# Router logits in a decoder layer: the tokens as the stationary operand, the eight router columns as the moving one

## The chip, the cores and the metric

The kernel runs on one core of one Trainium2 chip. The metric is the device time of one execution in microseconds (us). The core has a matrix engine (TensorE, PE in the rows; its weight loads are listed apart as PEld), a vector engine (VectorE, DVE), a scalar engine (ScalarE, ACT), GpSimd (POOL) and a sync engine (SyncE, SP) whose queue issues the transfers here. TensorE's array runs at one of two clocks, 1.2 or 2.4 GHz; the profile gives the granted clock as a share of full speed, 0.5 or 1.0.

A matmul on TensorE has a stationary operand, which a weight load (LDWEIGHTS) puts into the array, and a moving operand, whose columns stream through it.

## The reference

The reference is one decoder layer over 64 sequences of 128 tokens, 256 wide: self-attention and a norm, cross-attention and a norm, then a mixture of eight experts and a norm. The change lies in the first step of the mixture, the router's logits. There are 8192 tokens, and every token gets eight logits:

```python
N = B * T
x = x_btd.reshape(N, Dm)
cap = int(math.ceil(CF * N / E))
probs = jax.nn.softmax(x @ Wr + br, axis=-1)
gates, ids = jax.lax.top_k(probs, K)
```

`Wr` is 256x8 and `br` has 8 elements, all in float32. The two largest probabilities of a token pick its experts; each expert takes at most `cap` tokens, those with the largest gates.

## The kernel before

The program is a row of blocks, each with a program of its own for every engine and a common end: the attention layers (`attention_layers`), the logits (`logits_block`), the routing (`route_block`), the experts (`experts_block`) and the last norm (`norm_block`). A block starts when the one before it has ended on all engines, so what one block gains or loses in time is passed on to the end of the program unless a later one waits for something else.

`logits_block` takes the 8192 rows in 16 groups of 512 tokens (`G`), four tiles of 128 (`NB`). SyncE loads a group as a tile `x2` of 128 x 4 x 256 floats (512 KB); `LOADS` is the number of buffers, and load g waits until TensorE has transposed group g - LOADS (`t_full`). For each group g TensorE does three things:

- eight transposes (L845, `lg_T<-lg_ident,lg_x`), so that the features of a token lie across partitions. ScalarE and VectorE copy the two halves out of PSUM into `xT` (L866 and L885, 512 columns each);
- the logits, turned round (L825, `lg_L<-lg_xT,lg_wr`): the router's weight half `wr[:, t, :]`, eight columns, is stationary, and the 512 transposed tokens move; the two halves accumulate in `lb`, 8 partitions x 512. VectorE adds the bias, one number for each partition, and writes `lT` (L878);
- the way back (L834, `lg_B<-lg_ident,lg_lT`): four transposes of 8 x 128 that bring `lT` to 128 tokens x 8 logits in `bb`. ScalarE copies these 128x32 into `logits` (L861).

The order on TensorE is written out by hand as a pipeline: the transposes of group g, the logits of group g - 1 (`logits_of`), the way back of group g - 2 (`back`). TensorE works through its instructions in this order, and begins only when the two constants, `ident` and `wr`, and the bias are in (`const_in`). A matmul in float32 leaves two records in the trace, each with its own weight load, so a logits step of two matmuls has four; a transpose leaves one.

Of the kernel before, what the change touches and what calls it, by code (L numbers as in the profile page):

```python
# [4 lines left out]
FP32 = mybir.dt.float32  # L5
BF16 = mybir.dt.bfloat16
FP32R = mybir.dt.float32r
ALU = mybir.AluOpType
# [3 lines left out]
P = 128  # L12
# [3 lines left out]
NB = 4  # L16
G = NB * P
HALVES = D // P
# [745 lines left out]
E = 8  # L764
# [6 lines left out]
def logits_block(nc, tiles, rows_dram, sum_dram, wr_dram, br_dram, ident_dram, logits):  # L771


    groups = tiles // NB
    LOADS = 4
    with ExitStack() as c:
        ident = c.enter_context(nc.sbuf_tensor("lg_ident", [P, P], FP32))
        wr = c.enter_context(nc.sbuf_tensor("lg_wr", [P, HALVES, E], FP32))
        br = c.enter_context(nc.sbuf_tensor("lg_br", [E, 1], FP32))
        zero = c.enter_context(nc.sbuf_tensor("lg_zero", [P, D + E], FP32))  # L780
        x2 = c.enter_context(nc.sbuf_tensor("lg_x2", [P, LOADS, NB, D], FP32))
        xT = c.enter_context(nc.sbuf_tensor("lg_xT", [P, 2, HALVES, G], FP32))
        lT = c.enter_context(nc.sbuf_tensor("lg_lT", [E, 2, G], FP32))
        tb = [c.enter_context(nc.psum_tensor(f"lg_T{i}", [P, G], FP32)) for i in range(4)]
        lb = [c.enter_context(nc.psum_tensor(f"lg_L{i}", [E, G], FP32)) for i in range(2)]
        bb = [c.enter_context(nc.psum_tensor(f"lg_B{i}", [P, NB, E], FP32)) for i in range(2)]
        const_in = c.enter_context(nc.semaphore("lg_const_in"))
        x_loaded = [c.enter_context(nc.semaphore(f"lg_x_loaded{i}")) for i in range(LOADS)]
        zero_made = c.enter_context(nc.semaphore("lg_zero_made"))
        zeroed = c.enter_context(nc.semaphore("lg_zeroed"))  # L790
        t_full = c.enter_context(nc.semaphore("lg_t_full"))
        a_copied = c.enter_context(nc.semaphore("lg_a_copied"))
        d_copied = c.enter_context(nc.semaphore("lg_d_copied"))
        l_full = c.enter_context(nc.semaphore("lg_l_full"))
        l_done = c.enter_context(nc.semaphore("lg_l_done"))
        b_full = c.enter_context(nc.semaphore("lg_b_full"))
        b_done = c.enter_context(nc.semaphore("lg_b_done"))
        block = c.enter_context(nc.Block())

        @block.sync  # L800
        def _(sp):
            sp.dma_start(ident[:], ident_dram).then_inc(const_in, 16)
            sp.dma_start(wr[:], wr_dram.rearrange("(t p) n -> p t n", p=P)).then_inc(const_in, 16)
            sp.dma_start(br[:], br_dram.rearrange("(p a) -> p a", a=1)).then_inc(const_in, 16)
            for g in range(groups):
                if g >= LOADS:
                    sp.wait_ge(t_full, g - LOADS + 1)
                sp.dma_start(x2[:, g % LOADS], rows_dram[g * G:(g + 1) * G, 0:D]
                             .rearrange("(b p) n -> p b n", p=P)).then_inc(x_loaded[g % LOADS], 16)
            sp.wait_ge(zero_made, 1)  # L810
            sp.dma_start(rows_dram[groups * G:groups * G + P, :], zero[:]).then_inc(zeroed, 16)
            sp.dma_start(sum_dram[groups * G:groups * G + P, :], zero[:, 0:D]).then_inc(zeroed, 16)
            sp.wait_ge(zeroed, 32)

        @block.tensor
        def _(pe):
            pe.wait_ge(const_in, 48)

            def logits_of(g):
                pe.wait_ge(a_copied, g + 1)  # L820
                pe.wait_ge(d_copied, g + 1)
                if g >= 2:
                    pe.wait_ge(l_done, g - 1)
                for t in range(HALVES):
                    last = nc.tensor.matmul(lb[g % 2][:, :], wr[:, t, :], xT[:, g % 2, t, :],  # L825
                                            start=(t == 0), stop=(t == HALVES - 1))
                last.then_inc(l_full, 1)

            def back(g):
                pe.wait_ge(l_done, g + 1)  # L830
                if g >= 2:
                    pe.wait_ge(b_done, g - 1)
                for n in range(NB):
                    last = nc.tensor.matmul(bb[g % 2][:, n, :], lT[:, g % 2, n * P:(n + 1) * P], ident[0:E, 0:E],  # L834
                                            start=True, stop=True, is_transpose=True)
                last.then_inc(b_full, 1)

            for g in range(groups):
                pe.wait_ge(x_loaded[g % LOADS], 16 * (g // LOADS + 1))
                if g >= 2:  # L840
                    pe.wait_ge(a_copied, g - 1)
                    pe.wait_ge(d_copied, g - 1)
                for half in range(HALVES):
                    for n in range(NB):
                        last = nc.tensor.matmul(tb[2 * (g % 2) + half][:, n * P:(n + 1) * P],  # L845
                                                x2[:, g % LOADS, n, half * P:(half + 1) * P], ident[:],
                                                start=True, stop=True, is_transpose=True)
                last.then_inc(t_full, 1)
                if g >= 1:
                    logits_of(g - 1)  # L850
                if g >= 2:
                    back(g - 2)
            logits_of(groups - 1)
            back(groups - 2)
            back(groups - 1)

        @block.scalar
        def _(act):
            def take(g):
                act.wait_ge(b_full, g + 1)  # L860
                nc.scalar.copy(logits[:, g * NB:(g + 1) * NB, :], bb[g % 2][:, :, :]).then_inc(b_done, 1)  # L861
            for g in range(groups):
                act.wait_ge(t_full, g + 1)
                if g >= 2:
                    act.wait_ge(l_full, g - 1)
                nc.scalar.copy(xT[:, g % 2, 0, :], tb[2 * (g % 2)][:, :]).then_inc(a_copied, 1)  # L866
                if g >= 2:
                    take(g - 2)
            take(groups - 2)
            take(groups - 1)  # L870

        @block.vector
        def _(dve):
            def add_bias(g):
                dve.wait_ge(l_full, g + 1)
                if g >= 2:
                    dve.wait_ge(b_full, g - 1)
                nc.vector.tensor_scalar(lT[:, g % 2, :], lb[g % 2][:, :], br[:, 0:1], None, ALU.add).then_inc(l_done, 1)  # L878
            nc.vector.memset(zero[:], 0.0).then_inc(zero_made, 1)
            dve.wait_ge(const_in, 48)  # L880
            for g in range(groups):
                dve.wait_ge(t_full, g + 1)
                if g >= 2:
                    dve.wait_ge(l_full, g - 1)
                nc.vector.tensor_copy(xT[:, g % 2, 1, :], tb[2 * (g % 2) + 1][:, :]).then_inc(d_copied, 1)  # L885
                if g >= 1:
                    add_bias(g - 1)
            add_bias(groups - 1)
# [693 lines left out]
def moe(nc, tokens, cap, ins, rows, total, lists, out):  # L1582
    tiles = tokens // P
    with ExitStack() as c:
        logits = c.enter_context(nc.sbuf_tensor("logits", [P, tiles, E], FP32))
        logits_block(nc, tiles, rows, total, ins["wr"], ins["br"], ins["ident"], logits)
        route_block(nc, tiles, cap, logits, rows, lists, ins)
    experts_block(nc, cap, rows, lists, total, {k: ins[k] for k in ("w1", "w2", "b1", "b2")}, ins)
    norm_block(nc, tiles, total, out)
# [92 lines left out]
```

## Time and profile before

| | us |
|---|---|
| median of three runs | 1737.83 (1737.78 to 1737.97) |
| the profiled execution | 1737.31 |
| its span in the trace | 1735.6 |
| first load of x in the logits block issued | 983.28 |
| first transpose of the block | 987.07 |
| last write of logits begins | 1041.00 |
| first work of the routing block on VectorE | 1041.63 |

The page of the profile gives the whole span: TensorE is busy for 84% of it, VectorE for 61%, ScalarE for 56%. These shares mix stages with different limits. The logits block is about 3% of the span, and only its own stretch, from 982 to 1042 us, is read in what follows. Views used: the page; the timeline, which merges instructions of one kind in a row (start, duration of the merged piece, engine, line, operation, tile written <- tiles read, count, and in brackets the idle time before it and what ended it); the view of one tile's instructions; and the busy time of every engine by stretch with the granted clock. The durations of matmul records are modelled and contain the way through the array, so the spacing of their starts tells the rate, not their duration.

### The profile page before, as it was taken

Reading aid. Unit: us, or ns where it says so; the run is one execution under the profiler, and the core shown is the slowest. Engines: PE = TensorE matmul, PEld = TensorE weight load, DVE = VectorE, ACT = ScalarE, POOL = GpSimd, SP = SyncE. Lnnn points to the kernel's source line nnn. Section 1 sums busy time; section 2 is a strip of 40 time slices with the busy share of each in tenths; the row PEclk is TensorE's granted clock in tenths of the full one; section 3 lists DMA queues with packets and bytes.
Section 4 is the critical chain, followed back from the end, with each engine's and each line's share of the span. In section 5 each row is a group of like instructions: output and inputs, shape, how many; then the busy total and the mean of one; then the engine's idle time right before and its main releaser. Section 6 shows DMA issues by size and latency. Waiting matters only on the chain. (4 is left out here: it accounts for less than half of the span.)

```text
span 1735.6 us, 43611 instructions
## 1 busy us (share of the span) xinstructions
PE 1463.6 (84%) x17896; PEld 1214.8 (70%) x17896; DVE 1054.5 (61%) x2277; ACT 970.5 (56%) x1419; POOL 632.2 (36%) x615
## 2 busy tenths in 40 slices
PE   5999999999999999999998591223999999999950
PEld 4777777777777777777776341223999999999950
DVE  3666666666667677767766347794544454455425
ACT  3677767777766666676765220012655555555507
POOL 1544444444432222322230000055254455454326
PEclk9999999999999999999999795555999999999985
DMA  5011112112112222222111341004334433442229
GB/s 178 20 57 57 57 57 63 58 56 68 45 52 67 75 75 75 74 74 75 63 60 38 126 116 12 0 0 134 83 58 96 97 81 61 96 98 45 28 53 357
DMA packets 129795, 129.54 MB, mean 75 GB/s; under 512 B 28288, under 2 KB 116464, under 8 KB 129600
## 3 DMA queue, kind: packets, MB, share of 16 engines
q1 hardware_dynamic: 114496, 106.29, 19.6%
q0 software_dynamic: 15104, 20.48, 7.1%
q8 instruction: 143, 2.34, 0.5%
q14 instruction: 52, 0.43, 0.1%
HBM read 82.54 MB, written 44.20 MB: 73 GB/s over the span
## 5 line engine op out<-in xcount | busy, mean ns | idle before, releaser
L495 ACT ACTIVATE at_pr<-at_A 128x2048 f32<-128x2048 f32 x128 | 240.7, 1880 | 196.4 <-PE at_A L325 196.4
L587 DVE TENSOR_REDUCE at_mx<-at_A 128x12 f32<-128x1536 f32 x128 | 224.6, 1755 | 32.7 <-PE at_A L292 27.1
L34 PE MATMUL ex_D<-ex_w,ex_hT 128*128 128x256 f32 (+1 forms) x1920 | 233.8, 281 | 0.4
L34 PEld LDWEIGHTS ex_D<-ex_w,ex_hT 128*128 128x128 f32 (+1 forms) x1920 | 230.5, 184 | 3.1 <-DVE ex_raw L1426 1.9
L34 PE MATMUL ex_U<-ex_xT,ex_w 128*128 128x384 f32 (+1 forms) x1152 | 222.1, 352 | 0.0
L1482 POOL DMA_INDIRECT total<-ex_o,ex_ids x80 | 131.6, 1645 | 228.0 <-DVE ex_o L1431 196.3
L34 PEld LDWEIGHTS ex_U<-ex_xT,ex_w 128*128 128x128 f32 x1152 | 207.2, 189 | 7.4
L716 POOL TENSOR_SCALAR_AFFINE_SELECT at_pr<-at_pr 128x2048 f32<-128x2048 f32 x64 | 128.5, 2008 | 225.2 <-ACT at_pr L495 225.2
L1416 DVE TENSOR_TENSOR ex_hT<-ex_h,ex_hT 128x384 fp32r<-128x384 f32 (+1 forms) x192 | 112.6, 587 | 97.0 <-ACT ex_hT L1376 97.0
L623 DVE TENSOR_TENSOR at_oT<-at_C,at_oT 128x512 fp32r<-128x512 f32 x64 | 44.3, 692 | 178.0 <-ACT at_oT L508 178.0
L325 PE MATMUL at_A<-at_qp,at_kt 32*128 32x256 f32 x2048 | 142.5, 392 | 0.0
L341 PE MATMUL at_C<-at_pr,at_v 128*32 128x128 f32 x4096 | 139.2, 277 | 1.0 <-ACT at_oq L502 1.0
L341 PEld LDWEIGHTS at_C<-at_pr,at_v 128*32 128x32 f32 x4096 | 104.6, 110 | 43.7 <-issue 42.4
L1375 ACT ACTIVATE ex_h<-ex_U,ex_b 128x384 f32<-128x384 f32 (+1 forms) x192 | 116.7, 608 | 25.5 <-PE ex_U L34 21.4
L707 POOL TENSOR_TENSOR at_sT<-at_turned,at_sT 128x1024 fp32r<-128x1024 f32 x32 | 75.8, 2369 | 126.7 <-ACT at_sT L451 126.7
L1376 ACT ACTIVATE ex_hT<-ex_U,ex_b 128x384 fp32r<-128x384 f32 (+1 forms) x192 | 115.2, 600 | 0.0
L1466 POOL DMA_INDIRECT ex_xg<-rows,ex_ids x80 | 102.1, 1276 | 35.2 <-issue 22.6
L1348 ACT CAST ex_xT<-ex_T 128x384 fp32r<-128x384 f32 (+1 forms) x48 | 21.9, 510 | 165.4 <-PE ex_T L1299 165.4
L723 POOL TENSOR_SCALAR at_shift<-at_mv 128x2 f32<-128x2 f32 x64 | 14.8, 231 | 269.5 <-DVE at_mv L649 266.9
L34 PE MATMUL at_B<-at_wo,at_oT 128*128 128x256 f32 x768 | 108.1, 290 | 1.9 <-DVE at_oT L623 1.4
L34 PE MATMUL at_B<-at_sT,at_wk 128*128 128x512 f32 x384 | 105.8, 411 | 1.4 <-ACT at_qp L464 1.4
L34 PE MATMUL at_B<-at_wv,at_sT 128*128 128x256 f32 x768 | 106.7, 288 | 0.0
(189 smaller groups left out, 2703.3 us busy)
## 6 DMA issues: line engine op xcount, KB each, us to landing
ex_w_in<-in_w SPq DMA_DIRECT2D x16, 1024.0 KB, 6.8
at_turned<-in_x_turned SPq DMA_DIRECT2D x16, 512.0 KB, 4.0
at_x<-in_x SPq DMA_DIRECT2D x16, 512.0 KB, 3.7
x<-at_y SPq DMA_DIRECT2D x32, 256.0 KB, 2.2
at_x<-x SPq DMA_DIRECT2D x16, 512.0 KB, 3.7
at_turned<-in_ctx_turned SPq DMA_DIRECT2D x16, 512.0 KB, 4.1
rows<-at_y SPq DMA_DIRECT2D x32, 256.0 KB, 2.2
total<-at_y SPq DMA_DIRECT2D x32, 256.0 KB, 2.8
```

The source lines that it names most:

```text
L34: last = nc.tensor.matmul(out, pick_l(left, a), pick_r(right, b), start=(start and n == 0), stop=(stop and n == 2))
L325: last = nc.tensor.matmul(A[:, i, n, :, :], kt[rows, g % 2, half, tok], qp[rows, g % 2, half, :, tok], start=False, stop=(n == 1), skip_gr ...
L341: last = nc.tensor.matmul(b[32 * j:32 * j + VW, (2 * n + quad) * P:(2 * n + quad + 1) * P], v[:, g % 2, 2 * np_ + n, half * HEADS_HALF + 4 ...
L495: nc.scalar.activation(pr[:, k % 2].rearrange("p i n a q -> p (i n a q)"), A[:].rearrange("p i n a q -> p (i n a q)"), ACT.Exp).then_inc(e ...
L587: nc.vector.tensor_reduce(mx[:, k % 2, 0:12], A[:, 0:3].rearrange("p i n a k -> p (i n a) k"), AX, ALU.max).then_inc(max_done, 1)
L707: nc.gpsimd.tensor_tensor(sT[:, g % 2, 1], turned[:, g % 2], sT[:, g % 2, 0].bitcast(FP32), ALU.subtract).then_inc(s_lo, 1)
L716: nc.gpsimd.affine_select(out=t, in_=t, compare_op=ALU.is_ge, fill=0.0, base=0, pattern=[[0, 16], [1, P]], channel_multiplier=-1).then_inc ...
L1375: nc.scalar.activation(h[:, m % HR, 0:n], U[m % UP][:, 0:n], ACT.Silu, bias=b1[:, j, m:m + 1])
L1376: nc.scalar.activation(hT[:, par(j, ch), 0, m, 0:n], U[m % UP][:, 0:n], ACT.Silu, bias=b1[:, j, m:m + 1]).then_inc(u_done, 1)
L1416: nc.vector.tensor_tensor(hT[:, par(j, ch), 1, m, 0:n], h[:, m % HR, 0:n], hT[:, par(j, ch), 0, m, 0:n].bitcast(FP32), ALU.subtract).then_ ...
L1466: nc.gpsimd.indirect_dma_start(xg[0:n, xg_of(s), b, :], None, rows_dram, bass.IndirectOffsetOnAxis(ap=ids[0:n, e, at:at + 1], axis=0), bou ...
L1482: nc.gpsimd.indirect_dma_start(sum_dram, bass.IndirectOffsetOnAxis(ap=ids[0:n, e, at:at + 1], axis=0), o[0:n, pr, b, :], None, bounds_chec ...
```

## The change

The logits are computed the other way round. For each of the four 128-token tiles of a group and each half, the transposed tokens `xT[:, ., t, n*128:(n+1)*128]` (128x128) are stationary, and the eight columns of `wr` move. The result is 128 tokens x 8 logits at once, in `lb`, now 128 x 4 x 8. The way back (`back`, `bb`, `lT`, L834, L861) is gone with its semaphores; VectorE adds the bias, now spread over all partitions by the load, and writes straight to `logits`. Beside this `LOADS` goes from 4 to 6, and the first load of x is issued right behind that of `ident`, ahead of `wr` and `br`.

```diff
-    LOADS = 4
+    LOADS = 6
-        br = c.enter_context(nc.sbuf_tensor("lg_br", [E, 1], FP32))
+        br = c.enter_context(nc.sbuf_tensor("lg_br", [P, E], FP32))
-        lT = c.enter_context(nc.sbuf_tensor("lg_lT", [E, 2, G], FP32))
-        lb = [c.enter_context(nc.psum_tensor(f"lg_L{i}", [E, G], FP32)) for i in range(2)]
-        bb = [c.enter_context(nc.psum_tensor(f"lg_B{i}", [P, NB, E], FP32)) for i in range(2)]
+        lb = [c.enter_context(nc.psum_tensor(f"lg_L{i}", [P, NB, E], FP32)) for i in range(2)]
...
-                for t in range(HALVES):
-                    last = nc.tensor.matmul(lb[g % 2][:, :], wr[:, t, :], xT[:, g % 2, t, :],
-                                            start=(t == 0), stop=(t == HALVES - 1))
+                for n in range(NB):
+                    for t in range(HALVES):
+                        last = nc.tensor.matmul(lb[g % 2][:, n, :], xT[:, g % 2, t, n * P:(n + 1) * P], wr[:, t, :],
+                                                start=(t == 0), stop=(t == HALVES - 1))
                 last.then_inc(l_full, 1)
-
-            def back(g):
-                pe.wait_ge(l_done, g + 1)
-                if g >= 2:
-                    pe.wait_ge(b_done, g - 1)
-                for n in range(NB):
-                    last = nc.tensor.matmul(bb[g % 2][:, n, :], lT[:, g % 2, n * P:(n + 1) * P], ident[0:E, 0:E],
-                                            start=True, stop=True, is_transpose=True)
-                last.then_inc(b_full, 1)
...
-                nc.vector.tensor_scalar(lT[:, g % 2, :], lb[g % 2][:, :], br[:, 0:1], None, ALU.add).then_inc(l_done, 1)
+                nc.vector.tensor_tensor(logits[:, g * NB:(g + 1) * NB, :], lb[g % 2][:, :, :],
+                                        br[:, :].unsqueeze(1).to_broadcast([P, NB, E]), ALU.add).then_inc(l_done, 1)
```

How this stands on TensorE, at the start of the logits block, before the change (lines of the kernel before; `lg_T` the transposed tokens, `lg_L` the logits, `lg_B` the way back; the count is of matmuls in a row):

```order
L845 MATMUL lg_T<-lg_ident,lg_x 128x128 x16
L825 MATMUL lg_L<-lg_xT,lg_wr 8x512 x2
L845 MATMUL lg_T<-lg_ident,lg_x 128x128 x8
L825 MATMUL lg_L<-lg_xT,lg_wr 8x512 x2
L834 MATMUL lg_B<-lg_ident,lg_lT 128x8 x4
L845 MATMUL lg_T<-lg_ident,lg_x 128x128 x8
```

The same place on TensorE in the changed kernel, where the transposes stand on its line 836:

```order
L836 MATMUL lg_T<-lg_ident,lg_x 128x128 x16
L825 MATMUL lg_L<-lg_wr,lg_xT 128x8 x8
L836 MATMUL lg_T<-lg_ident,lg_x 128x128 x8
L825 MATMUL lg_L<-lg_wr,lg_xT 128x8 x8
L836 MATMUL lg_T<-lg_ident,lg_x 128x128 x8
```

Two matmuls of 512 moving columns and four small transposes have become eight matmuls of eight moving columns; the transposes of the tokens stand where they stood. On SyncE's queue, at the start of the block, the difference is this:

```order
-L802 DMA lg_ident<-in_ident 128x128
-L803 DMA lg_wr<-in_wr 128x2x8
-L804 DMA lg_br<-in_br 8x1
-L808 DMA lg_x<-rows 128x4x256 x16
...
+L803 DMA lg_ident<-in_ident 128x128
+L801 DMA lg_x<-rows 128x4x256
+L805 DMA lg_wr<-in_wr 128x2x8
+L806 DMA lg_br<-in_br 128x8
+L801 DMA lg_x<-rows 128x4x256 x15
```

The first load of x has moved two places ahead, and the bias is now fetched once for each partition.

## Rows read from the trace of the kernel before

**Rows 1.** The page: the span, and the granted clock in 40 slices.

```profile
span 1735.6 us, 43611 instructions
...
PEclk9999999999999999999999795555999999999985
```

**Rows 2.** The timeline, start of the block, SyncE's queue and TensorE (columns described above).

```profile
982.35 0.43 SPq L803 DMA_DIRECT2D lg_wr<-in_wr  x1
...
983.28 14.70 SPq L808 DMA_DIRECT2D lg_x<-rows  x8
...
987.07 3.65 PE L845 MATMUL lg_T<-lg_ident,lg_x 128*128 128x128 f32 x16 [13.11 <-DMA lg_x<-rows]
...
990.65 2.73 PE L825 MATMUL lg_L<-lg_xT,lg_wr 128*8 128x512 f32 x4
```

**Rows 3.** The timeline of TensorE, one turn in the middle of the block.

```profile
1002.86 1.09 PE L845 MATMUL lg_T<-lg_ident,lg_x 128*128 128x128 f32 x8
1003.88 1.88 PE L825 MATMUL lg_L<-lg_xT,lg_wr 128*8 128x512 f32 x4
1005.69 0.41 PE L834 MATMUL lg_B<-lg_ident,lg_lT 8*128 8x8 f32 x4
1006.03 1.09 PE L845 MATMUL lg_T<-lg_ident,lg_x 128*128 128x128 f32 x8
```

**Rows 4.** The tile view: count, ns min/median/max of one, first and last start.

```profile
L825 PE MATMUL lg_L<-lg_xT,lg_wr x64: 592/592/1057, 990.7 to 1039.1; 128*8 128x512 f32 x64
L878 DVE TENSOR_SCALAR lg_lT<-lg_L,lg_br x16: 737/739/740, 993.4 to 1039.8; 8x512 f32<-8x512 f32 x16
L885 DVE COPY lg_xT<-lg_T x16: 690/692/692, 989.1 to 1035.8; 128x512 f32<-128x512 f32 x16
```

**Rows 5.** The timeline, end of the block.

```profile
1034.65 1.09 PE L845 MATMUL lg_T<-lg_ident,lg_x 128*128 128x128 f32 x8
...
1041.00 0.18 ACT L861 COPY logits<-lg_B 128x32 f32<-128x32 f32 x1 [0.72 <-PE lg_B L834]
```

**Rows 6.** The routing block: float32 matmuls with 128x128 weights and two moving columns.

```profile
1124.88 0.57 PE L1007 MATMUL rt_C<-rt_tot,rt_same 128*128 128x2 f32 x2
...
L1007 PE MATMUL rt_C<-rt_tot,rt_same x2: 353/353/353, 1124.9 to 1125.1; 128*128 128x2 f32 x2
...
1125.48 0.16 DVE L1100 COPY rt_off<-rt_C 128x2 f32<-128x2 f32 x1 [1.11 <-PE rt_C L1007]
```

**Rows 7.** The timeline of weight loads in the experts block, 128x128, 256 moving columns each.

```profile
1304.49 5.82 PEld L34 LDWEIGHTS ex_D<-ex_w,ex_hT 128*128 128x128 f32 x48
```

**Rows 8.** Busy time by stretch, with the granted clock.

```profile
core 0: us, PE busy (x) PEld busy (x) DVE busy (x) ACT busy (x) POOL busy (x), PEclk, DMA share, GB/s
576.00:579.40 3.40, 2.03 (x30) 1.68 (x30) 2.57 (x5) 2.21 (x4) 2.36 (x1) 1.00 0.00 0
965.10:968.50 3.40, 1.40 (x13) 1.16 (x11) 2.54 (x8) 0.00 (x0) 0.45 (x2) 1.00 0.46 152
968.50:971.90 3.40, 1.98 (x8) 1.58 (x9) 0.69 (x1) 1.57 (x3) 0.90 (x2) 0.50 0.00 0
985.60:989.00 3.40, 1.93 (x9) 1.96 (x10) 0.00 (x0) 0.00 (x0) 0.00 (x0) 0.50 1.08 365
989.00:992.40 3.40, 3.40 (x12) 1.64 (x11) 1.38 (x2) 1.17 (x2) 0.00 (x0) 0.50 1.02 334
992.40:995.80 3.40, 3.40 (x15) 1.19 (x13) 1.43 (x2) 0.58 (x1) 0.00 (x0) 1.00 0.54 160
1006.03:1009.22 3.19, 3.19 (x19) 1.46 (x17) 1.44 (x3) 0.77 (x2) 0.00 (x0) 1.00 0.55 169
1061.00:1119.00 58.00, 16.89 (x58) 14.42 (x58) 40.88 (x201) 0.00 (x0) 0.00 (x0) 0.50 0.02 1
1140.00:1187.00 47.00, 18.32 (x128) 16.00 (x128) 42.02 (x19) 9.56 (x8) 33.14 (x8) 0.50 0.00 0
```

More of the change, by code:

```diff
@@ L795, in logits_block @@
         l_done = c.enter_context(nc.semaphore("lg_l_done"))
-        b_full = c.enter_context(nc.semaphore("lg_b_full"))
-        b_done = c.enter_context(nc.semaphore("lg_b_done"))
         block = c.enter_context(nc.Block())
@@ L801, in _, with load @@
         def _(sp):
[L802 to L805, printed above, removed]
+            def load(g):
                 if g >= LOADS:
@@ L809, in _ @@
                              .rearrange("(b p) n -> p b n", p=P)).then_inc(x_loaded[g % LOADS], 16)
+            sp.dma_start(ident[:], ident_dram).then_inc(const_in, 16)
+            load(0)
+            sp.dma_start(wr[:], wr_dram.rearrange("(t p) n -> p t n", p=P)).then_inc(const_in, 16)
+            sp.dma_start(br[:], br_dram.rearrange("(a n) -> a n", a=1).to_broadcast([P, E])).then_inc(const_in, 16)
+            for g in range(1, groups):
+                load(g)
             sp.wait_ge(zero_made, 1)
@@ L850, in _ @@
                     logits_of(g - 1)
-                if g >= 2:
-                    back(g - 2)
             logits_of(groups - 1)
-            back(groups - 2)
-            back(groups - 1)
         @block.scalar
         def _(act):
-            def take(g):
-                act.wait_ge(b_full, g + 1)
-                nc.scalar.copy(logits[:, g * NB:(g + 1) * NB, :], bb[g % 2][:, :, :]).then_inc(b_done, 1)
             for g in range(groups):
@@ L866, in _ @@
                 nc.scalar.copy(xT[:, g % 2, 0, :], tb[2 * (g % 2)][:, :]).then_inc(a_copied, 1)
[L867 to L870, printed above, removed]
         @block.vector
@@ L875, in add_bias @@
                 dve.wait_ge(l_full, g + 1)
-                if g >= 2:
-                    dve.wait_ge(b_full, g - 1)
-                nc.vector.tensor_scalar(lT[:, g % 2, :], lb[g % 2][:, :], br[:, 0:1], None, ALU.add).then_inc(l_done, 1)
+                nc.vector.tensor_tensor(logits[:, g * NB:(g + 1) * NB, :], lb[g % 2][:, :, :],
+                                        br[:, :].unsqueeze(1).to_broadcast([P, NB, E]), ALU.add).then_inc(l_done, 1)
             nc.vector.memset(zero[:], 0.0).then_inc(zero_made, 1)
```

## The prediction, made before the changed kernel ran

> **What bounds the kernel now.** I first looked at where the block lies in the whole. The span is 1735.6 us, and the granted clock of TensorE is near full speed except around 980 us and in the routing stage [rows 1]. The logits block runs from 983.28 (first load of x) to about 1041.2 (last write of logits) [rows 2, 5]. The routing block reads all the logits in its first reduction, so whatever the block gains or loses goes straight to the end of the program.
>
> Inside the block the timeline of TensorE is what to read. One turn in the middle takes 1006.03 - 1002.86 = 3.17 us: 1.02 from the first transpose to the first logits matmul, 1.81 for the logits, 0.34 for the way back [rows 3]. TensorE is busy for the whole of such a turn, VectorE for 1.44 us, ScalarE for 0.77, and the DMA engines for 0.55 of it [rows 8]. So TensorE's work is the bound, and nothing else is near. The two ends differ: the first 5.3 us of its work, to 992.4, run at a granted clock of 0.5 (1.2 GHz), the rest at 1.0 (2.4 GHz) [rows 8]; and behind the last transposes (1034.65) the chain logits, bias, way back, copy takes until 1041.18, 6.5 us [rows 5].
>
> **The way back, removed.** It costs 0.34 us in each turn [rows 3] and part of the tail. Nothing hides it now, so it is a gain in full. The bias add on VectorE shrinks from 0.739 us (8x512) [rows 4] to something like the 0.16 us of a 128x2 copy from PSUM [rows 6]; I take 0.2. VectorE then has 0.69 + 0.2 of work per turn, ScalarE only its copy; neither is waited for.
>
> **The logits, turned round.** Before, two matmuls, four records, each 512 columns: (1.88 - 0.59)/3 = 0.43 us apart at 2.4 GHz [rows 3, 4], so 1.72 us and a switch of about 0.09. After, eight matmuls, sixteen records, each with a weight load of 128x128 in float32 and eight moving columns. This kind of pair stands in the trace in one place, with two moving columns and at 1.2 GHz: (0.57 - 0.353) = 0.214 us apart [rows 6], at the low clock like the whole stretch just ahead of it [rows 8]. Since the columns can't take that long, this is the price of the load: 107 ns at 2.4 GHz, if it scales with the clock. That is the lower bound. The upper one is the down projection, where the same size of load has 256 columns beside it: 5.82/48 = 0.121 us [rows 7]. I take 0.107 + 0.007 = 0.114, adding the eight columns at the rate of the 512 (0.43 x 8/512 = 0.007 us). Then:
> - at 2.4 GHz: 16 x 0.114 + 0.09 = 1.91 us a turn (1.80 to 2.03), where there were 1.81 + 0.34 = 2.15. The gain is only 0.24 us a turn: the sixteen loads cost what the four long streams cost.
> - at 1.2 GHz: 16 x 0.214 + 0.10 = 3.52 us a turn.
>
> The Trainium skill, "TensorE: Matmul & The Clock Gate", section on LDWEIGHTS, puts a load of 128 columns at 128/1.2 = 107 ns whatever the clock. By that the sixteen loads would be 1.7 us also at 1.2 GHz, and the whole block would end near where it ends today. The trace disagrees for float32 at the low clock, 0.214 us, and the measurement decides.
>
> **Transposes.** Eight take 1.02 - 0.15 for the switch = 0.87 us at 2.4 GHz. At 1.2 GHz two groups and a switch took 990.65 - 987.07 = 3.58, so 1.71 a group [rows 2].
>
> **The loads.** The first load of x is issued where that of `wr` stood, 982.35 instead of 983.28: 0.93 us earlier [rows 2]. `wr` and `br` now queue behind its 512 KB, and TensorE waits for both, so I give back a little: first transpose at 986.3 instead of 987.07 (bounds 986.0 and 987.1). A load costs 0.512 MB / 365 GB/s = 1.4 us of the DMA engines, at the rate of 985.6 to 989.0 [rows 8], less than any turn below, with four buffers or with six. LOADS costs and brings nothing.
>
> **The clock decides the sign.** In a turn of the new block the moving columns take 0.87 us (transposes) and 16 x 0.007 = 0.11; the other 1.8 us are weight loads. Today the columns move nearly without a gap. What the rows show of the clock: it stood at 0.5 while the first transposes ran for 1.93 us of a 3.4 us stretch, and went to 1.0 at 992.4 behind a stretch filled with transposes and 512-column matmuls (3.40 of 3.40 busy). Earlier it fell at 968.5 behind a stretch with 13 matmuls and 1.40 us of TensorE busy, and did not rise behind one with 1.98 us. It stayed 0.5 all through the bit search of the routing block, 1061 to 1119, where TensorE's 16.9 us are almost nothing but float32 loads of 128x128 (14.4 us), and through 1140 to 1187 with 128 matmuls in 47 us [rows 8]. A stretch that is filled with loads and has few columns stands nowhere. If the loads count as work for the clock, TensorE is as busy as today, and the clock rises at about 992.4 and stays. If only moving columns count, the new block looks like the stretches at 0.5: transposes for a third of the time and next to nothing behind. Nothing in the trace decides it. I lean to the second: in each of these rows the clock can be read from the moving columns alone, and none needs the loads to explain it.
>
> **Forecast: the block runs at 1.2 GHz to its end.** TensorE starts at 986.3. Transposes of two groups and the switch 3.6; 16 logits steps x 3.42 = 54.8; 14 groups of transposes x 1.71 = 23.9; 28 switches x 0.1 = 2.8; the last matmul's way out, bias and end 0.35. Sum 85.5, so the end at 1071.8, against 1041.2: +30.6 us. The profiled execution took 1737.31, so 1767.9; it lies 0.5 below the median, so 1768.4 on that scale. Own range 1758 to 1771: one or two stretches at the high clock near the start would take 3 to 7 us off (the two first groups of transposes run back to back there), and 0.218 instead of 0.214 adds 1.
>
> **Rival 1: the loads keep the clock up.** The clock rises at 992.4 as today. By then two groups of transposes are done (989.9) and 2.5 us of the first logits; the other 1 us shrinks to 0.5, so the third group starts at 993.0, 0.3 ahead of today. A turn is 1.02 + 1.91 = 2.93 (2.82 to 3.05) against 3.17: 13 turns give 3.1 us. Behind the last transposes come 1.02 + 1.91 + 1.82 and 0.35 = 5.1 instead of 6.5: 1.4. Sum -4.8 us, 1733.0; with the bounds of the load, 13 x 0.12 and 2 x 0.12 either way, 1731 to 1735, and down to 1729.5 if the clock rises a stretch earlier. For it: TensorE has work without a gap from the first transpose to the last. Against: the bit search. The Trainium skill, same page, Part 1, says that the gate follows how busy the array has been lately, without saying whether a load is busyness; taken by its word, it is this rival. No run here shows it yet.
>
> **Rival 2: the clock goes up and down.** The transposes come in a block of 0.87 or 1.71 us in every turn, so a stretch may hold one or two of them, and some stretches may be granted 1.0. The time then lies between the two, some 1740 to 1757. The row from 576.0 to 579.4 speaks for it: 30 matmuls and 2.03 us, much of it idle, and the clock was 1.0 [rows 8]. Against it: a stretch of the new block at 0.5 holds one block of transposes, as the one from 985.6 did, which did not bring the clock up.
>
> **Rival 3: no measurable change.** Rival 1 with the load at 0.121, or a first transpose that comes no earlier because `br` and `wr` wait behind the 512 KB: both together leave -3 us, at the edge of what can be told from none (0.2%, 3.5 us, about what a measurement of this kernel can separate).
>
> **Chances.** Forecast 0.50. Rival 2 0.07. Rivals 1 and 3, the same clock as today, 0.43, of which 0.36 lie beyond 0.2% and 0.07 within. Slower by over 0.2%: 0.50 + 0.07, less 0.01 for a rival 2 near the level of today: 0.56. Faster 0.36, same 0.07 + 0.01 = 0.08. Both signs hold much; the range must reach from rival 1 to the top of the forecast: 1730 to 1771.
>
> **What would show each step.** The granted clock in the stretch 992 to 1070 is the first thing: 0.5 throughout for the forecast, 1.0 for rival 1. The spacing of the sixteen records of a logits step: 0.214 us at the low clock, 0.107 to 0.121 at the high one. The turn: 5.3 us or 2.9 us. No row of `lg_B`; the bias add near 0.2 us; the first transpose near 986.3. VectorE, ScalarE and DMA waiting for TensorE, never the other way. The forecast is wrong if the clock is 1.0 behind 993; the price of the load is wrong if the spacing lies outside 0.107 to 0.121 at that clock.

## The result and the profile after

| | us |
|---|---|
| changed kernel, median of four runs | 1764.93 (1763.50 to 1766.03) |
| before, in the same comparison | 1737.8 (1733.49 to 1737.97) |
| ratio | 1.0161, 95% interval 1.0144 to 1.0177 |
| profiled execution of the changed kernel | 1764.62, span 1762.9 |

The change makes the kernel slower by 27 us, 1.6%. The forecast of 1768.4, slower, held in sign and is 3.5 us too high.

The page of the changed kernel shows in one line what differs. Against [rows 1] the granted clock of TensorE no longer has its 7 and 9 in the slices of the logits block; it is at 5 there, as in the routing stage behind it.

```profile
span 1762.9 us, 43823 instructions
...
PEclk9999999999999999999999555555999999999985
```

The timeline of TensorE, start of the block and one turn in the middle, answers [rows 2] and [rows 3] (start and duration of the merged piece, engine, line, operation, tiles, form, count, idle time and what ended it):

```profile
986.51 1.97 PE L836 MATMUL lg_T<-lg_ident,lg_x 128*128 128x128 f32 x8 [12.85 <-DMA lg_br<-in_br]
...
989.69 1.97 PE L836 MATMUL lg_T<-lg_ident,lg_x 128*128 128x128 f32 x8 [1.21 <-DMA lg_x<-rows]
...
991.45 3.42 PE L825 MATMUL lg_L<-lg_wr,lg_xT 128*128 128x8 f32 x16
...
1006.49 3.42 PE L825 MATMUL lg_L<-lg_wr,lg_xT 128*128 128x8 f32 x16
1009.76 1.95 PE L836 MATMUL lg_T<-lg_ident,lg_x 128*128 128x128 f32 x8
1011.50 0.65 PE L825 MATMUL lg_L<-lg_wr,lg_xT 128*128 128x8 f32 x3
```

A turn takes 1011.50 - 1006.49 = 5.01 us instead of 3.17: 3.27 for the sixteen records of eight columns and 1.74 for the transposes, twice the 0.87 that they take at the high clock. The view by stretch shows that from 992 on TensorE and its weight loads are busy throughout, and the clock is 0.5 all the same:

```profile
core 0: us, PE busy (x) PEld busy (x) DVE busy (x) ACT busy (x) POOL busy (x), PEclk, DMA share, GB/s
988.60:992.00 3.40, 2.31 (x12) 2.31 (x12) 0.99 (x2) 0.81 (x2) 0.00 (x0) 0.50 1.09 384
1006.49:1011.50 5.01, 5.01 (x25) 5.01 (x25) 0.88 (x2) 0.59 (x1) 0.00 (x0) 0.50 0.37 105
992.00:1068.00 76.00, 76.00 (x365) 76.00 (x364) 12.94 (x30) 8.48 (x15) 0.00 (x0) 0.50 0.28 82
```

In one turn VectorE is down from 1.44 us [rows 8] to 0.88 and ScalarE from 0.77 to 0.59, so what the change was to save on them is saved, beside an engine that is full. The end of the block, against [rows 5]:

```profile
1068.51 0.19 DVE L856 TENSOR_TENSOR logits<-lg_L,lg_br 128x32 f32<-128x32 f32 x1 [3.22 <-PE lg_L L825]
1068.98 0.33 SPq L955 DMA_DIRECT2D rt_ident<-in_ident  x1
```

From here on a block's length is taken from the issue of its first transfer (`lg_ident`) to that of the routing block's (`rt_ident`), which leaves out what the attention layers do differently from one execution to the next. Before it is 59.5 us (981.96 to 1041.45), after 87.3 (981.66 to 1068.98): +27.8, and the spans differ by 27.3. The whole difference is in this block.

### The profile page after: what moved, and what is told of

It reads as the page before. It is cut to its first block and busy times, and to the rows that moved or that the text cites. A ratio compares the mean times of both kernels' runs of the same rounds, so it can differ in the third digit from the quotient of the medians.

```text
span 1762.9 us, 43823 instructions
## 1 busy us (share of the span) xinstructions
PE 1490.3 (85%) x18024; PEld 1269.4 (72%) x18024; DVE 1045.6 (59%) x2277; ACT 968.1 (55%) x1403; POOL 631.4 (36%) x615
## 5 line engine op out<-in xcount | busy, mean ns | idle before, releaser
L341 PE MATMUL at_C<-at_pr,at_v 128*32 128x128 f32 x4096 | 139.2, 277 | 1.0 <-ACT at_oq L502 1.0
L341 PEld LDWEIGHTS at_C<-at_pr,at_v 128*32 128x32 f32 x4096 | 104.6, 110 | 43.7 <-issue 42.4
```

Source lines behind the costliest of these rows:

```text
L341: last = nc.tensor.matmul(b[32 * j:32 * j + VW, (2 * n + quad) * P:(2 * n + quad + 1) * P], v[:, g % 2, 2 * np_ + n, half * HEADS_HALF + 4 ...
```

## The experiments

The theory: the granted clock follows the columns that move through the array, and weight loads don't hold it up, so a block whose time goes to loads runs at 1.2 GHz and every load costs twice what it does at 2.4 GHz. The rivals: the price lies in the float32 loads themselves, whatever moves; the block only missed the rise of the clock, by its cold start and the gap of 1.21 us; or the other part of the change, the loads of x, is to blame.

### More columns behind the same loads

```diff
-        lb = [c.enter_context(nc.psum_tensor(f"lg_L{i}", [P, NB, E], FP32)) for i in range(2)]
+        lb = [c.enter_context(nc.psum_tensor(f"lg_L{i}", [P, NB, 16, E], FP32)) for i in range(2)]
...
-                        last = nc.tensor.matmul(lb[g % 2][:, n, :], xT[:, g % 2, t, n * P:(n + 1) * P], wr[:, t, :],
+                        last = nc.tensor.matmul(lb[g % 2][:, n, :, :], xT[:, g % 2, t, n * P:(n + 1) * P],
+                                                wr[:, t, :].unsqueeze(1).to_broadcast([P, 16, E]),
...
-                nc.vector.tensor_tensor(logits[:, g * NB:(g + 1) * NB, :], lb[g % 2][:, :, :],
+                nc.vector.tensor_tensor(logits[:, g * NB:(g + 1) * NB, :], lb[g % 2][:, :, 0, :],
```

> The changed kernel with one edit: each of the sixteen logits records of a turn moves 128 columns instead of 8 (the eight router columns repeated 16 times), with the same sixteen weight loads; the extra results are not read. Theory (only moving columns hold the clock up): the granted clock goes to 1.0 at about 992 and stays, the records stand 0.107 to 0.121 us apart, a turn takes 2.8 to 3.1 us, and the time is 1731 to 1738 us, some 30 us less than the changed kernel with a sixteenth of the columns. Rival (the price is the float32 loads themselves, whatever moves; or their chain of waits): the time stays at 1765 or grows, the clock stays 0.5.

Measured: 1731.9 us (nine runs), ratio to before 0.9969 (0.9959 to 0.9979), so 33 us faster than the changed kernel, with sixteen times its columns in the logits, and a little faster than the kernel before. The block takes 53.5 us. The timeline of its TensorE, one turn, and the view by stretch:

```profile
998.82 1.03 PE L837 MATMUL lg_T<-lg_ident,lg_x 128*128 128x128 f32 x8
999.70 1.95 PE L825 MATMUL lg_L<-lg_wr,lg_xT 128*128 128x128 f32 x16
1001.48 1.03 PE L837 MATMUL lg_T<-lg_ident,lg_x 128*128 128x128 f32 x8
...
992.00:996.60 4.60, 4.60 (x24) 4.60 (x23) 0.88 (x2) 0.59 (x1) 0.00 (x0) 0.51 1.08 382
996.60:1035.00 38.40, 38.40 (x349) 38.40 (x348) 12.36 (x28) 8.19 (x14) 0.00 (x0) 1.00 0.44 125
```

TensorE counts as busy to the full in both kernels, with the same number of loads; what differs is the moving columns, and the clock with them. At the high clock the sixteen records take 1.78 us with 128 columns each, 0.111 apart. The columns alone would take about as much by estimate, 0.107 us, a quarter of the 0.43 us of 512 columns [rows 3, 4], so loads and columns run beside each other here. The rival of a price that the loads have whatever moves falls: the same loads stand half as far apart. Two expectations missed: the clock rose at 996.6 and not at about 992, which no run took apart, and a turn takes 1001.48 - 998.82 = 2.66 us, less than the 2.8 to 3.1 given. More moving columns also mean more multiplications and more results written to PSUM; no run here tells these apart.

### A warm start

```diff
+            def fill(times):
+                for _ in range(times):
+                    nc.tensor.matmul(junk[:, :], ones_b[:, 0:P], ones_b[:, :], start=True, stop=True)
+
+            pe.wait_ge(zero_made, 1)
+            fill(20)
             pe.wait_ge(const_in, 48)
```

> The changed kernel with 20 bfloat16 matmuls of 512 columns on a constant tile ahead of everything in the block, while TensorE would wait for the first load; they end some 2 to 4 us after the first load has landed. Theory (the loads don't hold the clock): it goes to 1.0 near 986 to 989, falls back within the next 10 us, and the time is 1758 to 1768. Rival (the clock was only missed because the block starts cold and with a gap; once up, the unbroken stream of loads keeps it): clock 1.0 to the end of the block, time 1733 to 1738.

Measured: 1759.37 us in one run, block 81.4 us. The timeline of TensorE (19 of the 20 wide matmuls are in the trace; the row from 993.99 is a narrower window and has thirteen of the sixteen records from 993.85, whose own duration is in the tile row) and the view by stretch:

```profile
983.23 6.12 PE L820 MATMUL lg_junk<-lg_ones_b 128*128 128x512 bf16 x19 [9.41 <-DVE lg_zero L867]
...
993.85 1.85 PE L833 MATMUL lg_L<-lg_wr,lg_xT 128*128 128x8 f32 x16
993.99 1.60 PE L833 MATMUL lg_L<-lg_wr,lg_xT 128*128 128x8 f32 x13
L833 PE MATMUL lg_L<-lg_wr,lg_xT x13: 256/256/256, 994.0 to 995.3; 128*128 128x8 f32 x13
995.55 1.07 PE L844 MATMUL lg_T<-lg_ident,lg_x 128*128 128x128 f32 x8
...
1000.79 3.42 PE L833 MATMUL lg_L<-lg_wr,lg_xT 128*128 128x8 f32 x16
...
987.00:990.40 3.40, 3.40 (x23) 2.24 (x22) 0.07 (x1) 0.14 (x1) 0.00 (x0) 1.00 0.95 328
990.40:993.80 3.40, 3.33 (x31) 3.12 (x30) 1.50 (x3) 1.03 (x2) 0.00 (x0) 1.00 1.09 385
993.80:997.20 3.40, 3.40 (x34) 3.40 (x32) 1.42 (x3) 1.13 (x2) 0.00 (x0) 1.00 1.08 376
997.20:1004.00 6.80, 6.80 (x34) 6.80 (x35) 1.04 (x3) 0.63 (x2) 0.00 (x0) 0.50 0.65 196
1004.00:1063.00 59.00, 58.77 (x281) 58.67 (x281) 10.10 (x24) 6.46 (x11) 0.00 (x0) 0.50 0.19 50
```

The clock was up when the block's own work began, and the sixteen records took 995.55 - 993.85 = 1.70 us, half of the 3.27 that they take in the changed kernel. It fell at 997.2 behind a stretch in which TensorE and its loads were busy from end to end (3.40 and 3.40 of 3.40). It had been up for 10.2 us (986.97 to 997.21) and did not rise again in the block. So loads without a gap don't hold it. The cold start costs some 6 us (the block 81.4 against 87.3) but isn't the cause.

### The same start with more columns, and without it

The changed kernel with 32 moving columns in each record instead of 8 (a broadcast of four), once as it is and once behind the twenty wide matmuls:

> The changed kernel with 32 moving columns in each logits record instead of 8 (128 brought the clock up): same loads. At the low clock the columns then take about half of the time of a turn, where they take a third with 8. Theory: the clock is set by the columns, but starting low this is still like the stretches that stayed low: clock 0.5, 1757 to 1767. If half of the time is enough to bring it up: 1732 to 1737.

> wide32 behind the 20 wide matmuls of warm_start. There the clock rose at 987 and fell again at 997, with 8 columns a record. Theory (the clock follows the moving columns, and holding it takes fewer than getting it): with 32 columns it rises at 985 to 990 and holds to the end of the block, 1731 to 1738, though the same block without the warm start stays low. Rival (the loads pull it down whatever the start): it falls within 10 us as in warm_start, 1757 to 1765.

Measured in one run each: 1764.97 and 1731.48 us, blocks of 87.2 and 50.4 us. The same turn of both, on TensorE, and a stretch of each. First wide32:

```profile
996.70 3.46 PE L825 MATMUL lg_L<-lg_wr,lg_xT 128*128 128x32 f32 x16
999.98 1.95 PE L837 MATMUL lg_T<-lg_ident,lg_x 128*128 128x128 f32 x8
1001.72 3.46 PE L825 MATMUL lg_L<-lg_wr,lg_xT 128*128 128x32 f32 x16
...
995.00:1066.00 71.00, 71.00 (x341) 71.00 (x342) 12.56 (x29) 8.20 (x14) 0.00 (x0) 0.50 0.26 73
```

Then warm_32:

```profile
1021.12 1.87 PE L833 MATMUL lg_L<-lg_wr,lg_xT 128*128 128x32 f32 x16
1022.82 1.07 PE L845 MATMUL lg_T<-lg_ident,lg_x 128*128 128x128 f32 x8
1023.73 1.87 PE L833 MATMUL lg_L<-lg_wr,lg_xT 128*128 128x32 f32 x16
...
1010.00:1030.00 20.00, 20.00 (x187) 20.00 (x185) 7.03 (x16) 4.68 (x8) 0.00 (x0) 1.00 0.32 91
```

One and the same stream of instructions runs at either clock: 5.02 us a turn where it began low, 2.61 where it began high. With eight columns the high clock was lost after 10 us; with 32 it was kept for 44 us, from 987.6 to 1031.9, and fell only in the last two logits steps, behind which no transposes come. With 32 columns, then, what the clock was before decided it; each side of this pair is one run.

### The parts apart

The first run takes the changed kernel and puts the loads back as they were:

```diff
-    LOADS = 6
+    LOADS = 4
...
             sp.dma_start(ident[:], ident_dram).then_inc(const_in, 16)
-            load(0)
...
-            for g in range(1, groups):
+            for g in range(groups):
                 load(g)
```

> The changed kernel with the order of the first transfers and the four buffers of the kernel before; only the orientation of the logits is changed. Theory: clock 0.5 all through, 1763 to 1767, within 1 us of the changed kernel; the first two groups of transposes run back to back again (1.2 us less idle) but start 0.4 to 0.9 later. Rival (two buffers more and the new order cause the loss, by the gap of 1.2 us between the first two groups of transposes): clock 1.0 from 992, 1733 to 1738.

The second takes the kernel before and gives it `LOADS = 6` and the new order of the first transfers, and nothing else:

> The kernel before with the other part of the change alone: six buffers for x, and the first load of x ahead of those of wr and br. Theory (this part moves the start by less than 1 us and nothing else, since TensorE waits for no load behind the first two groups): 1735.5 to 1738.5 against 1737.2 of before in the last comparison. Rival (six buffers let more loads in at once, and the second group comes so late that the clock rises a stretch later): 2 to 4 us slower.

Measured: the new orientation with the old loads takes 1763.05 us (four runs, 1757.79 to 1765.55; ratio 1.0143, 1.0119 to 1.0168; block 86.8 us), and the old orientation with the new loads 1737.98 (ratio 1.0005, 0.9996 to 1.0013; block 59.5 us, as before). The loss is in the orientation. The timeline of old_loads shows the first two groups back to back, without the gap, and the clock is 0.5 none the less (they start 5.80 us behind the block's first issue, against 4.85 in the changed kernel, 0.95 later where 0.4 to 0.9 was expected):

```profile
985.71 3.65 PE L835 MATMUL lg_T<-lg_ident,lg_x 128*128 128x128 f32 x16 [13.79 <-DMA lg_x<-rows]
989.15 3.42 PE L824 MATMUL lg_L<-lg_wr,lg_xT 128*128 128x8 f32 x16
...
992.00:1066.00 74.00, 74.00 (x355) 74.00 (x355) 12.56 (x29) 8.19 (x14) 0.00 (x0) 0.50 0.28 78
```

In only_loads TensorE began 4.9 us behind the block's first issue (983.62 to 988.54), against 5.1 in the kernel before (981.96 to 987.07). It was held by `br`, which had been put behind the first 512 KB, so the earlier load of x gained next to nothing:

```profile
988.54 3.92 PE L848 MATMUL lg_T<-lg_ident,lg_x 128*128 128x128 f32 x16 [12.91 <-DMA lg_br<-in_br]
```

### Fewer loads and more columns at once

If columns hold the clock and the loads of 128x128 are the price, the old orientation is the right one, and its long streams can be split and run beside each other: one product of the attention stage of this kernel (`at_C<-at_pr,at_v`, L341) does so with four groups of 32 of the array's columns, each with output partitions of its own. This kernel starts from the one before:

```diff
                 for t in range(HALVES):
-                    last = nc.tensor.matmul(lb[g % 2][:, :], wr[:, t, :], xT[:, g % 2, t, :],
-                                            start=(t == 0), stop=(t == HALVES - 1))
+                    for n in range(NB):
+                        last = nc.tensor.matmul(lb[g % 2][CG * n:CG * (n + 1), :], wr[:, t, :], xT[:, g % 2, t, n * P:(n + 1) * P],
+                                                start=(t == 0), stop=(t == HALVES - 1), skip_group_check=True)
...
-                for n in range(NB):
-                    last = nc.tensor.matmul(bb[g % 2][:, n, :], lT[:, g % 2, n * P:(n + 1) * P], ident[0:E, 0:E],
-                                            start=True, stop=True, is_transpose=True)
+                nc.tensor.matmul(bb[g % 2][:, :, :].rearrange("p n c -> p (n c)"), lT[:, g % 2, :], ident[:],
+                                 start=True, stop=True, is_transpose=True).then_inc(b_full, 1)
```

`CG` is 32; `wr` is padded to 32 columns with zeros, `br` is loaded once for each group of partitions, and ScalarE takes the first eight columns of each 32.

> The kernel before in its own orientation (router columns stationary, tokens moving), but the four token tiles of a group go to four column groups of the array, 32 output partitions each, so that four matmuls of 128 columns run beside each other; the weights are padded to 32 columns with zeros, the bias add is 128x128, and the way back is one transpose of 128x128 instead of four. Theory (columns are streamed nearly all the time): clock 1.0 as before from about 992; the logits step takes 0.45 to 0.6 us instead of 1.72, a turn 1.7 to 2.1 us instead of 3.17, the time 1713 to 1722. Rival (so few columns per load and so many loads bring the clock down here too): clock 0.5, a turn above 3 us, 1735 or more.

Measured: 1714.86 us (four runs), ratio to before 0.9870 (0.9854 to 0.9887): 22 us faster than before and 50 faster than the change. The block takes 37.0 us. Its timeline, one turn on TensorE, and the bias add; then the view by stretch:

```profile
1004.47 0.65 PE L830 MATMUL lg_L<-lg_xT,lg_wr 128*32 128x128 f32 x16
1005.05 0.33 PE L838 MATMUL lg_B<-lg_ident,lg_lT 128*128 128x128 f32 x1
1005.21 1.04 PE L848 MATMUL lg_T<-lg_ident,lg_x 128*128 128x128 f32 x8
1006.18 0.65 PE L830 MATMUL lg_L<-lg_xT,lg_wr 128*32 128x128 f32 x16
1006.90 0.35 DVE L881 TENSOR_SCALAR lg_lT<-lg_L,lg_br 128x128 f32<-128x128 f32 x1
...
988.50:992.70 4.20, 4.17 (x28) 3.84 (x32) 1.18 (x2) 1.08 (x2) 0.00 (x0) 0.50 1.07 338
...
1000.00:1010.00 10.00, 9.95 (x149) 7.75 (x147) 5.23 (x12) 4.34 (x12) 0.00 (x0) 1.00 0.97 305
```

The logits step takes 0.58 us instead of 1.81, the way back 0.16 instead of 0.34, the bias add 0.35 instead of 0.74, a turn 1.71 instead of 3.17. The rival of many loads falls here too: sixteen loads a step, of 32 columns each, with columns moving beside them, and the clock is 1.0 from 992.7. The DMA engines are now busy for 0.97 of the stretch. Whether the loads of x already bound the block is what the next run asks.

> column_tiles with six buffers for x instead of four. With four, a turn took 1.71 us and the DMA engines were busy for 0.97 of the stretch. Theory (TensorE's own work of 1.71 us a turn is still the bound, the loads just keep up): within 1.5 us of column_tiles, 1713 to 1716. Rival (TensorE waits for loads there, deeper buffers help): 2 to 4 us less.

Measured: 1716.63 us (four runs), ratio 0.9886 (0.9871 to 0.9901), block 36.8 us against 37.0. That is 0.6 us above the range expected; the intervals of the two ratios overlap, and the block is not longer. Deeper buffers bring nothing, though the DMA engines are as full as they are: TensorE's 1.71 us a turn is still what bounds, and in the whole block of column_tiles it waits once for a load behind its start, for 0.2 us.

## Why the prediction was right, step by step

- **What bounds.** TensorE's order did, before and after; no other engine was waited for behind the first two groups.
- **The sign hung on the clock, and the step held for the reason given.** It had been left open by the trace of before (0.50 against 0.43 for the same clock as today), so the forecast was a lean that came true and not a derivation. The runs wide128, warm_start and the pair with 32 columns settle it: the clock is not held by loads.
- **The load at the low clock**: forecast 0.214 us, measured 0.213. The row from 1006.77 below shows thirteen of the sixteen records of a step, each 0.361 long by the tile view above it: (2.92 - 0.361)/12. The subtraction as the prediction prints it, 0.57 - 0.353, gives 0.217 and not 0.214; the value used was the better one. **At the high clock**: forecast 0.107 to 0.121, taken 0.114, measured (1.60 - 0.256)/12 = 0.112 in warm_start with 8 columns and 0.111 in wide128 with 128. So the load cost what was forecast at both clocks.
- **The first gap of a step was missed.** The third record of a step stands 1006.77 - 1006.49 = 0.28 us behind the first, where two gaps of 0.213 would be 0.43. The first gap is thus only about 0.07, and a step takes 3.27 us instead of 16 x 0.214 = 3.42. No kernel looked into why; the second of the last two steps, with no transposes ahead of it, has no such gap (32 records in 6.83 us are 30 gaps of 0.213, one of 0.07, and the last record).

```profile
L825 PE MATMUL lg_L<-lg_wr,lg_xT x256: 218/361/361, 991.5 to 1068.1; 128*128 128x8 f32 x128
1006.77 2.92 PE L825 MATMUL lg_L<-lg_wr,lg_xT 128*128 128x8 f32 x13
...
991.24 3.53 PEld L825 LDWEIGHTS lg_L<-lg_wr,lg_xT 128*128 128x128 f32 x16
...
1061.63 6.83 PE L825 MATMUL lg_L<-lg_wr,lg_xT 128*128 128x8 f32 x32
```

- **The switches, 28 x 0.1 us, were mis-sized.** They were carried over from [rows 3]. The turn was forecast at 5.3 us and is 5.01; over 14 turns that is 4.5 us: 2.8 of the switches and 2.1 of the shorter logits steps, less 0.4 because the transposes take 1.74 and not 1.71. The 3.27 us of the logits and the 1.74 of the transposes add up to the turn with no gap between them: the next load starts ahead of the last matmul (the loads of the first logits step start at 991.24, the matmuls at 991.45).
- **The start.** First transposes forecast at 986.3, measured 986.51, held by `br` as written. Missed: "LOADS costs and brings nothing" left out that the second group's load comes late. TensorE waited 1.21 us for it, and the first logits step began at 991.45 instead of 989.9: 1.5 us. With the old loads this wait is gone (old_loads); whether the six buffers or the order makes it was not tested. With 4.5 less and 1.5 more the block ends 3.1 us ahead of the forecast 1071.8, at 1068.7, which is nearly the whole error of 3.3 us against the profiled execution. The two errors went opposite ways, so that the sum came out closer than its terms is in part luck.
- **The bias add**: forecast 0.2, measured 0.19.
- **Rival 1** had the block right in direction for the high clock, and its turn too long: 2.93 us, where warm_start and warm_32 take 2.61 at that clock, for the same two reasons (the switches and the first gap). It would have given a block of 54.7 us (59.5 - 4.8); wide128 and warm_32, which ran at that clock for most of the block, took 53.5 and 50.4. **Rival 2**, a clock that goes up and down, stands in no trace: in warm_start it was up for 10 us, fell and stayed down. **Rival 3** hung on rival 1's clock and fell with it.
- The Trainium skill, page "TensorE: Matmul & The Clock Gate", section on LDWEIGHTS, gives P / 1.2 ns for P columns, by which 128 columns are estimated at 107 ns whatever the clock. The float32 load of this kernel is near that at the high clock (0.112 us) and takes twice as long at the low one (0.213).

## What to carry to other kernels

Before turning a matmul round so that a narrow operand moves, count the weight loads and the moving columns: here sixteen float32 loads of 128x128 cost 1.7 us at 2.4 GHz, what two matmuls of 512 columns had cost, so little was to be won; and with eight columns moving behind each load, TensorE was full and ran at 1.2 GHz, where they cost 3.3. A share of busy time near 100% doesn't say that the clock is up; read the granted clock beside it. In this kernel it was better to keep the narrow operand stationary and to run four streams beside each other in column groups: with the shorter way back that comes with it, that took 22 us off.

## What the runs showed of the hardware that was not expected

- The same instructions ran at 0.5 for the whole block or at 1.0 for nearly all of it, by the clock at which they began: 5.02 and 2.61 us a turn, 1764.97 and 1731.48 us.
- Adding work that is thrown away made the kernel 33 us faster (128 moving columns instead of 8), since it hid behind the loads and brought the clock up.
- Sixteen float32 records of 128 columns in four column groups took 0.58 us together; one 512-column record takes 0.43.
- The transfer of the first 512 KB, moved ahead of two small ones, gained nothing (ratio 1.0005): TensorE then waited for one of the small ones (`br`), and in the changed kernel 1.21 us more for the second group.
